# Block 0 of a residual stack: both sequences ahead of the expert stream instead of one, and products of x for 14 sequences instead of 12

## What is computed

```python
# layer 0: 16 decays, per sequence
ctx = causal_ema(x, tau_ctx)
gated = x * sigmoid([x, ctx] @ Wg.T + bg)
h1 = gelu(x @ Wn1.T + bn1)
mod = 0.5 + sigmoid(h1 @ Wn2.T + bn2)                       # 16 columns
traces = causal_ema(gated * mod[..., d], tau[d])            # d = 0..15
temporal = sum_d traces[d] * softmax(blend)[d]
soma = gelu(x @ Wsoma.T + bsoma)
x = x + layernorm((soma * sigmoid(temporal @ Wtemp.T + btemp)) @ Wout.T) * gamma + beta
# layer 1: attention pooling with one of three masks by the prompt's type
x = x + pool(x, W1, b1, v, type)
# layer 2: 8 experts and a shared one, hidden width 1024
x = x + sum_e coef[e] * ((silu(x @ Wg[e]) * (x @ Wu[e])) @ Wd[e])
# layer 3: a shared head of 1024, and one of 8 small output experts
x = x + [gelu(x @ W1 + b1) @ W2 + b2, gelu(x @ W1 + b1) @ We[i] + be[i]]
```

## Time and profile before

| | |
|---|---|
| median of 3 runs | 2899.25 us (2899.01 to 2901.66) |
| the profiled execution | 2903.88 us |
| its span (first to last instruction) | 2902.1 us |
| PE busy | 2840.9 us, 98% |
| VectorE, ScalarE, GpSimd busy | 1805.6, 1373.3, 1212.6 us |
| mean granted clock of TensorE | 0.993 of full speed |

### The profile page before, as it was taken

The page is one execution under the profiler, slowest core; times in us unless marked ns, Lnnn a source line. Parts: engine busy times, 40 slices in busy tenths (PEclk is TensorE's granted clock), DMA queues, the critical chain, the costliest instruction groups (busy, mean ns, idle before and its releaser), DMA issues.

```text
span 2902.1 us, 37391 instructions
## 1 busy us (share of the span) xinstructions
PE 2840.9 (98%) x13414; PEld 2368.5 (82%) x13414; DVE 1805.6 (62%) x3018; ACT 1373.3 (47%) x2420; POOL 1212.6 (42%) x950
## 2 busy tenths in 40 slices
PE   8799999999999999999999999999999999999998
PEld 5587879888888888888888888888888888888887
DVE  6679777777655686656666567556655556334443
ACT  3334644464345453456335454357533446334544
POOL 4317335534543355434454235533444433333333
PEclk9999999999999999999999999999999999999999
DMA  5232232122111132113111112112111113111331
GB/s 185 84 120 91 88 96 71 54 80 72 50 48 55 53 90 63 48 43 104 44 44 48 55 55 80 48 48 70 58 55 50 48 56 96 50 44 52 117 98 39
DMA packets 84312, 199.63 MB, mean 69 GB/s; under 512 B 10136, under 2 KB 26400, under 8 KB 84128
## 3 DMA queue, kind: packets, MB, share of 16 engines
q1 hardware_dynamic: 80992, 188.74, 21.3%
q0 software_dynamic: 2560, 8.39, 0.9%
q10 hardware_dynamic: 576, 0.11, 0.0%
HBM read 189.67 MB, written 7.54 MB: 68 GB/s over the span
## 4 chain that ended last, share of the span: by engine, by line
PE 93%; DVE 3%; ACT 2%; issue 2%; POOL 1%; DMA 0%; SPq 0%; DVEq 0%; ACTq 0%; POOLq 0%
PE bank L582 19%; PE bank L584 19%; PE bank L583 19%; PE ps_out L582 9%; PE ps_out L584 9%; PE ps_out L583 9%; PE bank L575 3%; PE ps_out L575 1%; PE bank L656 1%; PE ps_out L760 1%; DVE w_lo L1200 0%; DVE trace L1123 0%; DVE trace L1131 0%; DVE acc L1255 0%; PE bank L704 0%
## 5 line engine op out<-in xcount | busy, mean ns | idle before, releaser
L1372 POOL TENSOR_TENSOR hid_lo<-hid,hid_hi 128x512 fp32r<-128x512 f32 (+1 forms) x640 | 847.8, 1325 | 1522.7 <-ACT hid_hi L1010 1522.3
L582 PE MATMUL bank<-res_lo,w_hi 128*128 128x512 f32 (+1 forms) x2432 | 948.3, 390 | 4.6 <-issue 3.5
L584 PE MATMUL bank<-res_hi,w_hi 128*128 128x512 f32 (+1 forms) x2432 | 938.2, 386 | 0.0
L583 PE MATMUL bank<-res_hi,w_lo 128*128 128x512 f32 (+1 forms) x2432 | 937.6, 386 | 0.0
L1229 DVE TENSOR_TENSOR hid<-hid,bank 128x512 f32<-128x512 f32 (+1 forms) x608 | 398.6, 656 | 582.7 <-PE bank L584 525.2
L981 ACT ACTIVATE hid<-bank 128x512 f32<-128x512 f32 (+1 forms) x608 | 349.3, 574 | 754.2 <-PE bank L584 676.4
L1200 DVE TENSOR_TENSOR w_lo<-w_raw,w_hi 128x768 fp32r<-128x768 f32 (+1 forms) x488 | 456.9, 937 | 185.6 <-ACT w_hi L944 139.5
L584 PEld LDWEIGHTS bank<-res_hi,w_hi 128*128 128x128 f32 x2432 | 458.5, 189 | 96.4
L582 PEld LDWEIGHTS bank<-res_lo,w_hi 128*128 128x128 f32 x2432 | 459.1, 189 | 93.0 <-issue 5.7
L583 PEld LDWEIGHTS bank<-res_hi,w_lo 128*128 128x128 f32 x2432 | 459.3, 189 | 81.8
L944 ACT ACTIVATE w_hi<-w_raw 128x768 fp32r<-128x768 f32 x360 | 304.4, 846 | 460.4 <-PE ps_out L584 453.0
(11 more groups left out here) (188 smaller groups left out, 1822.7 us busy)
## 6 DMA issues: line engine op xcount, KB each, us to landing
w_raw<-in_chunks SPq DMA_DIRECT2D x360, 384.0 KB, 3.0
w_raw<-in_head_chunks SPq DMA_DIRECT2D x64, 224.0 KB, 2.5
plain<-in_chunks SPq DMA_DIRECT2D x32, 384.0 KB, 3.6
x_in<-in_xT SPq DMA_DIRECT2D x16, 256.0 KB, 3.5
out_yT<-acc SPq DMA_DIRECT2D x8, 512.0 KB, 2.8
pre_x<-in_xT SPq DMA_DIRECT2D x12, 256.0 KB, 7.6
soma_rows<-pre_soma SPq DMA_DIRECT2D x12, 256.0 KB, 2.0
soma<-soma_rows SPq DMA_DIRECT2D x12, 256.0 KB, 3.1
```

The costliest lines, as they stand in the source:

```text
L582: mm(out, wh, xl, start=start and i == 0, stop=False, skip_group_check=not lone)
L583: mm(out, wl, xh, start=False, stop=False, skip_group_check=not lone)
L584: last = mm(out, wh, xh, start=False, stop=end, skip_group_check=not lone)
L1372: nc.gpsimd.tensor_tensor(hid_lo[i % DEPTH][:, tok], hid[i % 3][:, tok], f(hid_hi[i % DEPTH][:, tok]), ALU.subtract).then_inc(s_hlo, 1)
```

## The change

Block 0 is handled like the others in the stream: nine runs for both sequences in the exact form, `JOIN[0]` = 0, no lone steps, no `plain` buffers. So both sequences' side work stands ahead of the first step, in turns written by hand (`turns0`): sequence 1 follows sequence 0 by five pieces. `PRE` is 7, so 14 sequences have their products of x made there: two parts after nearly every turn in the 16 decays. Four chunks (`EARLY`) are cut in the tail of that lead, and the first third of the side weights (`part0`). The points at which blocks join move to 9, 16, 20, 26, 30, 36, 40, from 10, 14, 20, 24, 30, 34, 40. Steps go from 672 to 640, cuts from 424 to 456. The diff, cut to its core:

```diff
-LONE = 4
-NLONE = LONE * FC
-JOIN = [0, 10, 14, 20, 24, 30, 34, 40]
-LAST = [JOIN[b] + NE + (LONE if b == 0 else 0) for b in range(NBLK)]
+JOIN = [0, 9, 16, 20, 26, 30, 36, 40]
+LAST = [j + NE for j in JOIN]
...
-PRE = 6
+PRE = 7
...
-PARTS_AT = {j: 2 for j in range(7, 23)} | {11: 3, 13: 3, 15: 3, 22: 5, 24: 2, 27: 1, 28: 1, 34: 2, 35: 2, 36: 2}
+EARLY = {29: 0, 32: 1, 37: 2, 43: 3}
...
-    if i < NLONE:
-        return 2.1
-    if STEPS[i][4] is not None:
-        return 0.8
     return 2.4 if FIRST_USE[STEPS[i][3]] == i else 3.4
...
-    first = [0, 2, 4, 5, 6, 7, 8, 3] + list(range(9, PIECES))
-    fill = {11: 1, 12: 1, 13: 1, 15: 1, 17: 1, 22: 2, 28: 2, 36: 1, 40: 1, 44: 1}
+    turns0 = [(0, j) for j in (4, 5, 6, 7)] + [(1, 2), (0, 8), (0, 3), (1, 3), (0, 9), (1, 4), (0, 10), (1, 5), (0, 11), (1, 6)]
+    for j in range(12, PIECES):
+        turns0 += [(0, j), (1, j - 5)]
+    turns0 += [(1, j) for j in range(PIECES - 5, PIECES)]
...
+        for _ in range((1 if j < 12 and s == 0 else 2) if 7 <= j < 7 + ND else 0):
             if parts:
                 out.append(("pre", *parts.pop(0)))
...
+        if s == 0 and j == 40:
+            out.append(("setup", "part0"))
+        if s == 0 and j in EARLY:
+            out += [("cut", EARLY[j]), ("cut_lo", EARLY[j])]
...
-                while cut < len(CHUNKS) and ((cut_after(cut) is None and i >= 4 * cut + 4) or cut_after(cut) in backs):
+                while cut < len(CHUNKS) and ((cut_after(cut) is None and i >= cut - 3) or cut_after(cut) in backs):
...
-            def front_plain(i):
...
-            def back_plain(i):
...
-                if (b, kind) == (0, "experts"):
-                    activate(res_hi[0][:, :, 0:S], lone_x, ACT.Copy)
-                    activate(res_hi[0][:, :, S:BT], acc[0][:, :, S:BT], ACT.Copy).then_inc(s_rhi, 1)
-                else:
-                    activate(res_hi[slot][:], acc[b % NACC][:], ACT.Copy).then_inc(s_rhi, 1)
+                activate(res_hi[slot][:], acc[b % NACC][:], ACT.Copy).then_inc(s_rhi, 1)
```

More of the change, by code:

```diff
@@ L38 @@
         RUNS.append((k % (NE + 1), members(k)))
-    RUNS += [(HEAD, [(b, None)]) for b in range(NBLK) if k == LAST[b] + 1]
+    RUNS += [(HEAD, [b]) for b in range(NBLK) if k == LAST[b] + 1]
 WSLOTS = 9
@@ L133, in order @@
             out.append(("setup", "bias"))
-        for _ in range(fill.get(j, 0)):
-            out.append(("side", 0, 1, ahead))
-            ahead += 1
+        if s == 0 and j == 40:
+            out.append(("setup", "part0"))
+        if s == 0 and j in EARLY:
+            out += [("cut", EARLY[j]), ("cut_lo", EARLY[j])]
     rest = []
@@ L142, in order @@
     had = [0.0, LAG]
-    for s, n in ((0, PIECES), (1, ahead)):
+    for s, n in ((0, PIECES), (1, PIECES)):
         had[s] += sum(side_cost(b, j) for b, _, j in lanes[s][:n])
@@ L150, in order @@
         rest.append((b, s, j))
-    ready = [max(k for k, x in enumerate(rest) if x[0] == b) for b in range(NBLK)]
-    res = {0: 1}
+    ready = [max(k for k, x in enumerate(rest) if x[0] == b) if b else -1 for b in range(NBLK)]
+    res = {0: BB}
     occupant, turns = [None, None], [
@@ L203, in order @@
     for r, (e, blocks) in enumerate(RUNS):
-        while r >= LONE and res.get(blocks[-1][0], 0) < BB:
+        while res.get(blocks[-1], 0) < BB:
             piece()
-        for b, s in blocks:
+        for b in blocks:
             for c in range(FC):
@@ L209, in order @@
                 split_ready(i)
-                if r >= LONE and (b, kind) not in split:
+                if (b, kind) not in split:
                     if queue:
@@ L275, in stages_in @@
         return stages
-    plain = [x for x in stages if x not in SPLITS]
+    plain = [x for x in stages if x not in SPLITS and not (s and x == "alpha")]
     if s == 0 and "soma" in plain:
@@ L543, in _ @@
                 load_pre(u)
-            for n in range(PSLOTS):
-                fetch_plain(n)
             for n in range(NRAW):
@@ L1030, in _ @@
                     front(x[1])
-                elif x[0] == "late" and x[1] >= NLONE:
+                elif x[0] == "late":
                     late(x[1])
@@ L1188, in side @@
                         dve.wait_ge(s_y[b % NACC], 16 * (b // NACC))
-                    if b == 0 and s:
+                    if b == 0:
                         done("lo0")
-                    TT(lone_x if lead else acc[b % NACC][:, :, s * S:(s + 1) * S], both, x1[:],
-                       ALU.add).then_inc(l_dve[s], 1)
+                        dve.wait_ge(l_pe[1], pe_at(1, 0, "gate"))
+                    TT(acc[b % NACC][:, :, s * S:(s + 1) * S], both, x1[:], ALU.add).then_inc(l_dve[s], 1)
             def cut(n):
@@ L1249, in back @@
                     else:
[L1250 removed]
+                        for s in range(BB):
                             q, tok = b * BB + s, slice(s * S, (s + 1) * S)
```

157 lines of the change are left out of this document (50 added, 107 removed).

## The result

The changed kernel takes **2882.11 us** in the median of four runs (2880.28 to 2885.2), against 2900.35 us for the kernel before on the same chip: ratio 0.9935, interval 0.9923 to 0.9946. That is 18.2 us faster. The forecast was 2877, its range 2858 to 2898. The profiled span is 2883.4 us against 2902.1.

What follows compares the result with a forecast made beforehand. TensorE, busy 98% of the span, was taken as the bound. Lead +31.4, work -35.3 and idle time -18.7 sum to -22.6 us: 2879.5 on the profiled span, 2877 on the median, range 2858 to 2898.

Steps and rivals of the forecast that it cites:

- Part 1: Stream: TensorE work falls by the sum of (a), (b) and (c), 35.3 us, all of which counts.
- (a): Block 0 in the stream: 72 pair steps replace its lone, pair and second-sequence steps, -20.8 us.
- (b): Stream: what was left of block 0's second sequence at the first lone step goes ahead of it, -9.3 us.
- (c): Stream: block 7's two sequences no longer make their products of x there, -5.2 us.
- Part 2: Lead, now holding both sequences: the stream starts at 133 instead of 101.6, +31.4 us (bounds +23 to +44).
- the walk of the tail: Tail of the lead: second sequence followed from last scan to split with earlier durations, 39.6 us at full clock.
- Part 3: Stream's start to 450 us: idle and slow-clock time falls from 26.7 to 8 us, -18.7 us.
- (1): Stream: idle time stays in new places, only 3 us gained in place of 18.7, 2893 us; chance 0.16.
- (2): Lead: the two sequences' tails run in series, stream starts at 165, 2909 us; chance 0.09.
- (3): Lead shorter and idle time nearly gone: start at 125, 24 us regained, 2863 us; chance 0.13.
- (4): Lead's tail: each table switch costs 1.4 us more than its row, seven on the way, 2887 us; chance 0.04.
- (5): Lead: added products of x not hidden, +7.6 us, 2884 us; chance included in the main case's 0.58.

Runs made afterwards that it cites:

- the three edits: Changed kernel with head steps' budget 0.8, no dummy activations and 33 added float32 products in the lead: 2866.6 us; the same with PRE = 6: 2871.73 us.
- the repeated one: The changed kernel run again with no edit, beside the kernel before: 2881.46 us, ratio 0.9933.

## Why the prediction was right, and what was off

The forecast sum was 31.4 - 35.3 - 18.7 = -22.6 us on the span. Measured: +28.2 for the start, -46.9 for the stream, together -18.7.

**Part 1, the work: right.** Of the stream's -46.9 us, the idle and half-clock time up to 450 accounts for -19.8 and the idle time after 450 for +8.4 (below). What is left is -35.5, against -35.3. The instructions fit: 12644 rows of PE in the stream in place of 13119, and the 475 fewer are what (a), (b) and (c) add up to (384, 51 and 40). Term (c), 5.2 us for block 7's products of x, was tried apart, by the run of the three edits without them: 5.1.

**Part 2, the lead: right within its bounds, by errors that partly cancel, which is luck.** The stream was put at 133, and came at 129.9 and 126.7. The terms of the last scan add up to 88.7 and were written as 88.5. The last scan ended at 90.8 and not 88.5; the tail took 39.1 us and not 44.5. The kernel with the added products shows both at full clock: its last scan ends at 86.3, and its tail takes 36.2 us to 122.4. So DVE's turns were priced 2.2 us too dear, and so was the walk of the tail (39.6 at full clock) by 3.4; the 128x1024 `side_lo` took 1.22 us here where the row of before had 2.20. Against that kernel the changed one, at a clock of 0.74 from 70 to 90, lost 4.5 us in the decays of this execution, for which the prediction had nothing (the repeated one had its last scan at 87.2), and 2.9 in the tail, for which it had 5. The run with the joins of before bears it out for the decays: it has no added products, a clock of 1.00 from 70 to 80, and its last scan ends at 86.4. PE was busy 21.7 of 39 us there at a clock of 0.82, near the forecast 60% at under 0.9 (it is 56%). That DVE has no gaps from 32 to 80 held only roughly: 46.25 of 48 us.

**Part 3, the idle time at the stream's start: right.** 8 us were to be left in 300. In 320 it is 3.7 of idle PE and, at a clock of 0.99, about 3.2 more: 6.9, where it was 26.7 before. The long wait forecast for a modulation row did not show in PE's gaps.

**The step that failed** is the sentence behind part 3, "After that I change nothing: the pattern of heads and joins is of the same kind." That idle time was not kept: from 450 to the end it grew from 19.0 to 27.4 us. The windows of before gave a hint: DVE is busy 255 of 350 us between 450 and 800, and the change adds 32 cuts to DVE and puts a fuller schedule beside the first heads. A head step is short, 12 products of PE and not 18, but the planner gave it the side work of a full one, and a mean of 80% over 400 us hides 20 us at 99.5%. The edit of the head steps' budget gained 7.1 us, and the profiles agree: 20.0 us idle from 450 on in place of 27.4. Most of that is the first head; the 4 to 5 us around the second one stayed. PE waits for DVE in all of its gaps there, but what delays DVE is open. The forecast on the median is 5.1 us low: 7.1 from the stream, less 3.2 from the start, and 1.1 by which the kernel before was slower in the runs beside it (2900.35 against 2899.25).

**The rivals.** (1) The idle time stays, in new places: it put 15.7 us on that, and 8.4 came true, not at the start but later, half of it at the first head and half around the second. (2) Tails in series would start the stream at 165; it started at 130. (3) A start at 125 with the idle time gone: one profiled execution with the same lead began at 125.4, none had its stream. (4) The dearer table switch: the rows at 96.21, 98.46 and 100.61 above last 1.28 us each, and the next activation begins 1.29 to 1.30 us after each load's start, like the earlier trace rows. The drain of about 1.38 us that the Trainium skill (ScalarE: Activation LUTs, "What ACT_TABLE_LOAD costs") adds to a switch does not show in this trace either. The run without two of the loads agrees within its noise: 2 to 3 us gained, where 2 x 1.28 is 2.6. (5) The two added sets are hidden in the changed lead: of the two kernels with three edits, the one without the sets (PRE = 6) had its last scan end at 87.0, not before the 86.1 of the one with them, and its stream began at 121.3, not before 120.3. In the kernel before they are not, 7.0 us. The same edit is free or not by which engine limits the stage.

## What to carry to other kernels

A stage that is bound by a chain of small steps can cost the matmul engine time twice, by its gaps and by a lower clock (0.82 in the tail here). Independent work placed in the gaps, even work that nobody reads, took 5.2 us off here. Where a change fills the schedule of a second engine, look at that engine's share in windows of 20 us at the fullest places, not of 400: the mean hides the queue. Where a block leaves a pipeline, see that another one is in it for the next run, or its last stage waits with nothing to cover it. And moving work off the critical engine's path to an earlier stage gains its full time only if another engine limits that stage, as the same edit showed with 5.1 us gained in one kernel and 3.8 lost in the other.

## What was unexpected of the hardware

A DVE subtraction of two float32 tiles of 128x768 took 9.75 us in place of its 0.95. It stands in the same place, with the same 9.75, in the kernels with the added products and without the dummy activations, so it is no accident of one execution. In four long cases looked at singly POOL was working without a gap, and the DVE instruction ended 0.8 us after POOL's run did: 518.26 after a run to 517.45, in the kernel with the smaller budget 508.25 after 507.43, in the one with the later gather 538.70 after 537.87, and in the kernel before 1071.8. There the row of DVE is

```profile
1063.83 7.98 DVE L1200 TENSOR_TENSOR w_lo<-w_raw,w_hi 128x768 fp32r<-128x768 f32 x1
```

and the last row of POOL's run, with the one behind it:

```profile
1069.71 1.28 POOL L1372 TENSOR_TENSOR hid_lo<-hid,hid_hi 128x512 fp32r<-128x512 f32 x1
1072.11 1.30 POOL L1372 TENSOR_TENSOR hid_lo<-hid,hid_hi 128x512 fp32r<-128x512 f32 x1 [1.12 <-ACT hid_hi L1010]
```

POOL's run ends at 1070.99, DVE's instruction at 1071.81. The Trainium skill (GPSIMD Engine Reference, "1. Specifications") states that GpSimd shares its SBUF interfaces with VectorE and contends with DVE instructions that have two SBUF inputs. This subtraction is one, and the trace agrees; here such an instruction takes up to ten times its own duration. It is not always so: the subtractions of 64 columns beside the same kind of run, shown for the kernel with the later gather, came through about one per POOL instruction, every 1.25 us. Why a wide one has to wait for the end of the run, and not for the next POOL instruction, stays open.

It was also not expected that the lead scatters with the clock. Five profiled executions have the same instructions ahead of the stream. Their streams began at 129.9, 127.7, 127.1, 126.7 and 125.4, and their granted clocks from 70 to 80 were 0.73, 0.79, 0.83, 0.83 and 1.00 in that order. PE was busy 7.8 of those 10 us in each.
